# Cross-attention kernel: the value projection moved ahead of the queries, and the first queries in two alternating banks

## The reference, cut to what matters

```
q = split_heads(x @ Wq.T);  k = split_heads(ctx @ Wk.T);  v = split_heads(ctx @ Wv.T)
probs = softmax(q @ k.T / sqrt(32))
out = merge_heads(probs @ v) @ Wo.T + bo + x
```

## Time and profile before

| | |
|---|---|
| median of three executions | 444.74 us |
| profiled execution, its own time | 445.5 us |
| its span, first to last instruction | 443.7 us |
| TensorE busy | 432.1 us (97%) |
| VectorE busy | 314.3 us (71%) |
| ScalarE busy | 250.7 us (57%) |
| GpSimd busy | 228.2 us (51%) |

### The profile page before, as it was taken

How to read it: one execution, slowest core, us unless ns; L and a number is a source line. 1 busy time by engine, 2 the same in 40 slices (tenths; PEclk the granted TensorE clock), 3 DMA queues, 4 the chain that set the end, 5 groups by cost and what they waited for, 6 DMA issues and landing times.

```text
span 443.7 us, 8269 instructions
## 1 busy us (share of the span) xinstructions
PE 432.1 (97%) x2538; PEld 313.7 (71%) x2538; DVE 314.3 (71%) x509; ACT 250.7 (57%) x509; POOL 228.2 (51%) x184
## 2 busy tenths in 40 slices
PE   8989989899999999999999999999999999999996
PEld 6967665576777767776777766777777766777675
DVE  0465896877869586967869586967869586966663
ACT  1728876846565464756565464756565464755510
POOL 7403796836546373636546373636546373634440
PEclk9999989999999999999999999999999999999999
DMA  8995433535344534445344534455345443445203
GB/s 286 398 394 161 160 101 127 192 123 189 121 143 164 178 136 145 173 180 195 120 144 160 178 139 144 169 182 194 123 143 166 154 157 120 148 154 177 73 24 120
DMA packets 39615, 72.70 MB, mean 164 GB/s; under 512 B 5024, under 2 KB 6176, under 8 KB 39584
## 3 DMA queue, kind: packets, MB, share of 16 engines
q1 hardware_dynamic: 28784, 52.62, 33.2%
q10 hardware_dynamic: 10800, 19.67, 13.9%
HBM read 28.81 MB, written 10.49 MB: 89 GB/s over the span
## 4 chain that ended last, share of the span: by engine, by line
PE 91%; DVE 3%; ACT 2%; issue 1%; DMA 1%; POOL 1%; DVEq 0%; ACTq 0%; POOLq 0%
PE ps_q L676 30%; PE ps_o L676 26%; PE ps_s L722 9%; PE ps_pv L729 6%; PE ps_m L708 6%; PE ps_den L734 4%; PE ps_m L773 1%; DMA q_packed<-mxT 1%; PE ps_s L647 1%; PE ps_m L713 1%; PE ps_o L660 1%; PE ps_q L773 1%; ACT p_f L415 1%; PE ps_q L639 1%; DVE x_f L573 1%
## 5 line engine op out<-in xcount | busy, mean ns | idle before, releaser
L325 POOL TENSOR_TENSOR p_lo<-p_f,p_hi 77x512 f16<-77x512 f32 x120 | 147.7, 1236 | 169.6 <-ACT p_hi L419 169.6
L415 ACT ACTIVATE p_f<-ps_s 77x512 f32<-77x512 f32 x160 | 95.0, 593 | 47.4 <-PE ps_s L722 47.4
L419 ACT ACTIVATE p_hi<-ps_s 77x512 f16<-77x512 f32 x160 | 93.9, 587 | 1.0 <-PE ps_den L734 0.8
L534 DVE TENSOR_REDUCE mx<-ps_m 128x4 f32<-128x308 f32 x160 | 68.8, 471 | 18.0 <-PE ps_m L708 17.5
L676 PE MATMUL ps_q<-x_hi,wq_hi 128*128 128x512 f32 x200 | 79.9, 399 | 0.0
L676 PE MATMUL ps_q<-x_hi,wq_lo 128*128 128x512 f32 x200 | 78.5, 393 | 0.0
L676 PE MATMUL ps_q<-x_lo,wq_hi 128*128 128x512 f32 x200 | 78.5, 392 | 0.0
L527 DVE TENSOR_TENSOR q_lo<-ps_q,q_hi 128x512 fp32r<-128x512 f32 x40 | 27.6, 690 | 68.7 <-ACT q_hi L398 68.7
L398 ACT CAST q_hi<-ps_q 128x512 fp32r<-128x512 f32 x40 | 23.4, 585 | 91.8 <-PE ps_q L676 91.8
L676 PE MATMUL ps_o<-attn_hi,wo_hi 128*128 128x512 f32 x170 | 69.5, 409 | 0.0
L676 PE MATMUL ps_o<-attn_lo,wo_hi 128*128 128x512 f32 x170 | 66.9, 394 | 0.0
(11 more groups left out here) (105 smaller groups left out, 602.5 us busy)
## 6 DMA issues: line engine op xcount, KB each, us to landing
q_packed<-q_hi SPq DMA_DIRECT2D x80, 256.0 KB, 2.5
x_f<-in_x SPq DMA_DIRECT2D x40, 256.0 KB, 3.1
q_packed<-q_lo SPq DMA_DIRECT2D x40, 256.0 KB, 3.2
x_res<-in_x ACTq DMA_DIRECT2D x35, 256.0 KB, 2.8
out<-out_sb ACTq DMA_DIRECT2D x35, 256.0 KB, 2.6
wk_sb<-in_wk SPq DMA_DIRECT2D x8, 320.0 KB, 5.2
wv_sb<-in_wv SPq DMA_DIRECT2D x5, 512.0 KB, 10.9
wq_sb<-in_wq SPq DMA_DIRECT2D x5, 320.0 KB, 9.0
```

The costliest lines, as they stand in the source:

```text
L325: nc.gpsimd.tensor_tensor(p_lo[:, i, :], p_f[:, i, :], p_hi[:, i, :], ALU.subtract).then_inc(plo_pool, 1)
L415: nc.scalar.activation(p_f[:, i, :], ps_s[i % 2][0:L, :], ACT.Exp, scale=SCALE).then_inc(pf_done, 1)
L419: nc.scalar.activation(p_hi[:, i, :], ps_s[i % 2][0:L, :], ACT.Exp, scale=SCALE).then_inc(phi_done, 1)
L534: nc.vector.tensor_reduce(mx[:, g % RS, :, tt], ps_m[tt % 2][:, 0:HG * L].rearrange("p (h k) -> p h k", k=L), AX_X, ALU.max).then_inc(max_ ...
```

## The change

All five groups of v are projected directly behind the keys, each into a bank of its own (ps_m0, ps_m1, ps_q, ps_o, ps_pv), with their scaling, transposes and splitting interleaved; vT gets two buffers. The queries of (0, 0) come behind them. The DMA order puts two groups of Wv ahead of Wq's first group and the other three behind the first block of x. ScalarE and VectorE do the key split first at the start, then the first group of Wq. For pairs 0 to 7 the queries alternate between ps_q and ps_o. In the filling steps whose query group isn't group 0, the query chunks are spread: chunk 0 before the maxima's scores, chunk 1 behind them, chunk 2 behind the first scores, chunk 3 behind the second pair of maxima's scores, chunk 4 behind `transpose_max`. ScalarE does `q_high` ahead of the last exponentials in the filling steps. Nothing else is changed: `query_group` and the places where Wq's further groups are split remain.

```diff
@@ -75,10 +75,6 @@
...
         return isinstance(t, int) and t * G + g <= G
-
-    def value_group(t, g):
-
-        return (nth(t, g) + 1,) if isinstance(t, int) and -1 <= nth(t, g) < G - 1 else ()
...
@@ -190,7 +186,7 @@
...
             ctx_sb = sb("ctx_sb", [P, CC, BL], F32, start_up)
-            vT = sb("vT", [P, BL], F32, start_up)
+            vT = sb("vT", [P, 2, BL], F32, start_up)
         attn_hi = sb("attn_hi", [P, G, TB], F32R)
...
@@ -205,8 +201,14 @@
...
         ps_k = [ps_s[0], ps_s[1], ps_pv, ps_den, ps_o]
-        ps_v, ps_vt = ps_o[:, 0:BL], ps_o[0:L, 512 - B * P:512]
+        v_banks = [ps_m[0], ps_m[1], ps_q, ps_o, ps_pv]
+        ps_v = [v[:, 0:BL] for v in v_banks]
+        ps_vt = [v[0:L, 512 - B * P:512] for v in v_banks]
         ps_last = [ps_q, ps_m[0], ps_m[1], ps_o, ps_s[0]]
+
+        def query_bank(t, g):
+
+            return ps_o if isinstance(t, int) and t <= 1 and nth(t, g) < G + RS and nth(t, g) % 2 == 1 else ps_q
...
@@ -256,12 +258,19 @@
...
                 sp.dma_start(wk_sb[:, c, :], wk[:, c, :]).then_inc(wk_in[c], 16)
+
+            def load_wv(g):
+                sp.dma_start(wv_sb[:, g, :], wv[:, g, :]).then_inc(wv_in[g], 16)
+
+            load_wv(0)
+            load_wv(1)
             for g in range(G):
...
                     load_x(0, range(G))
+                    for v in range(2, G):
+                        load_wv(v)
                     sp.dma_start(bias[:, :], bo).then_inc(bias_in, 16)
-                sp.dma_start(wv_sb[:, g, :], wv[:, g, :]).then_inc(wv_in[g], 16)
             sp.wait_ge(const_done, 1)
...
@@ -389,13 +398,13 @@
...
                 nc.scalar.copy(v_hi[:, :, P * g:P * (g + 1)],
-                               ps_vt.rearrange("l (b c) -> l b c", b=B)).then_inc(vhi_done, 1)
+                               ps_vt[g].rearrange("l (b c) -> l b c", b=B)).then_inc(vhi_done, 1)
...
                     act.wait_ge(s_done, HG * (nth(*slot_before(t, g)) + 1))
-                nc.scalar.copy(q_hi[:, g % RS, :], ps_q[:, :]).then_inc(qhi_done, 1)
+                nc.scalar.copy(q_hi[:, g % RS, :], query_bank(t, g)[:, :]).then_inc(qhi_done, 1)
...
@@ -439,10 +448,17 @@
...
+            start_k()
             w_high(wq_in, wq_sb, wq_hi, wq_hi_done, (0,))
-            x_high(0, range(G))
-            start_k()
-            diagonal_k(0, range(HG))
+            x_high(0, range(0, 3))
+            v_high(0)
+            x_high(0, range(3, G))
+            v_high(1)
+            diagonal_k(0, range(0, 2))
+            v_high(2)
+            diagonal_k(0, range(2, HG))
+            v_high(3)
+            v_high(4)
...
@@ -458,17 +474,17 @@
...
                     exponentials(t, g, 2)
-                for v in value_group(t, g):
-                    v_high(v)
                 if exists(shift(t, g, 1)[0]):
                     copy_max(*shift(t, g, 1))
+                if filling(t, g):
+                    q_high(*shift(t, g, 2))
                 if exists(t):
...
                 attn_high(at, [c for c in (4,) if c in chunks])
-                if exists(shift(t, g, 2)[0]):
+                if exists(shift(t, g, 2)[0]) and not filling(t, g):
                     q_high(*shift(t, g, 2))
...
@@ -501,7 +517,7 @@
...
                 dve.wait_ge(vproj_done, g + 1)
-                nc.vector.tensor_reduce(v_scale[:, g:g + 1], ps_v, AX_X, ALU.max,
+                nc.vector.tensor_reduce(v_scale[:, g:g + 1], ps_v[g], AX_X, ALU.max,
                                         apply_absolute_value=True).then_inc(vscale_done, 1)
...
@@ -509,11 +525,13 @@
...
                 dve.wait_ge(vscale_done, 3 * g + 3)
-                nc.vector.tensor_scalar(vT[:, :], ps_v, v_inv[:, g:g + 1], None, ALU.mult).then_inc(vT_done, 1)
+                if g >= 2:
+                    dve.wait_ge(vtr_done, B * (g - 1))
+                nc.vector.tensor_scalar(vT[:, g % 2, :], ps_v[g], v_inv[:, g:g + 1], None, ALU.mult).then_inc(vT_done, 1)
...
                 dve.wait_ge(vhi_done, g + 1)
-                nc.vector.tensor_tensor(v_lo[:, :, P * g:P * (g + 1)], ps_vt.rearrange("l (b c) -> l b c", b=B),
+                nc.vector.tensor_tensor(v_lo[:, :, P * g:P * (g + 1)], ps_vt[g].rearrange("l (b c) -> l b c", b=B),
                                         v_hi[:, :, P * g:P * (g + 1)], ALU.subtract).then_inc(vlo_done, 1)
...
@@ -524,7 +542,7 @@
...
                 dve.wait_ge(qhi_done, nth(t, g) + 1)
-                nc.vector.tensor_tensor(q_lo[:, g % RS, :], ps_q[:, :], q_hi[:, g % RS, :].bitcast(F32),
+                nc.vector.tensor_tensor(q_lo[:, g % RS, :], query_bank(t, g)[:, :], q_hi[:, g % RS, :].bitcast(F32),
                                         ALU.subtract).then_inc(qlo_done, 1)
...
@@ -584,9 +602,20 @@
...
                                     AX_X, ALU.max).then_inc(mask_done, 1)
+            start_k()
             wq_low((0,))
-            x_low(0, DVE_CHUNKS)
-            start_k()
+            scale_v(0)
+            x_low(0, DVE_CHUNKS[:1])
+            scale_v(1)
+            v_low(0)
+            x_low(0, DVE_CHUNKS[1:])
+            scale_v(2)
+            v_low(1)
+            scale_v(3)
+            v_low(2)
+            scale_v(4)
+            v_low(3)
+            v_low(4)
             dve.wait_ge(bias_in, 16)
...
@@ -596,8 +625,6 @@
...
                     x_low(xt, DVE_CHUNKS[:1])
-                for v in value_group(t, g):
-                    scale_v(v)
                 if exists(shift(t, g, 1)[0]):
...
@@ -608,8 +635,6 @@
...
                     x_low(xt, DVE_CHUNKS[1:])
-                for v in value_group(t, g):
-                    v_low(v)
                 if exists(last_t):
...
@@ -651,13 +676,11 @@
...
-                if g == 0:
+                if g == RS:
                     pe.wait_ge(klo_done, G)
-                else:
-                    pe.wait_ge(vlo_done, g)
                 pe.wait_ge(wv_in[g], 16)
                 for c in range(CC):
-                    last = nc.tensor.matmul(ps_v, wv_sb[:, g, P * c:P * (c + 1)], ctx_sb[:, c, :],
+                    last = nc.tensor.matmul(ps_v[g], wv_sb[:, g, P * c:P * (c + 1)], ctx_sb[:, c, :],
                                             start=(c == 0), stop=(c == CC - 1))
...
@@ -665,7 +688,7 @@
...
                 for b in range(B):
-                    nc.tensor.transpose(ps_vt[:, P * b:P * (b + 1)], vT[:, L * b:L * (b + 1)],
+                    nc.tensor.transpose(ps_vt[g][:, P * b:P * (b + 1)], vT[:, g % 2, L * b:L * (b + 1)],
                                         ident[:, :]).then_inc(vtr_done, 1)
...
@@ -692,9 +715,11 @@
...
                         wait_chunk(xhi_done, xlo_dve, xlo_pool, t, c)
-                if 0 in chunks and exists(shift(t, g, -1)[0]):
+                if 0 in chunks and isinstance(t, int) and 2 <= nth(t, g) < G + RS:
+                    pe.wait_ge(qlo_done, nth(t, g) - 1)
+                elif 0 in chunks and exists(shift(t, g, -1)[0]):
                     pe.wait_ge(qlo_done, nth(t, g))
-                project(ps_q, wq_hi, wq_lo, x_hi, x_lo, g, chunks, ready, q_chunks)
+                project(query_bank(t, g), wq_hi, wq_lo, x_hi, x_lo, g, chunks, ready, q_chunks)
...
@@ -754,6 +779,8 @@
...
                     pe.wait_ge(outs_done, nth(t, k))
+                elif chunks[0] == 0:
+                    pe.wait_ge(qlo_done, G + RS)
                 project(out_bank(t, k), wo_hi, wo_lo, attn_hi, attn_lo, k, chunks, ready, o_chunks)
...
@@ -789,41 +816,51 @@
...
                 if (t, g) == (-1, G - 2):
-                    project_q(*query, range(G))
+                    project_v(0)
+                    project_v(1)
+                    for v in range(2, G):
+                        transpose_v(v - 2)
+                        project_v(v)
+                    transpose_v(3)
+                    pe.wait_ge(vlo_done, 3)
+                    project_q(*query, range(0, 2))
+                    transpose_v(4)
+                    project_q(*query, range(2, G))
                     return
...
                     pe.wait_ge(diag_done, HG)
-                    pe.wait_ge(klo_done, G)
-                for v in value_group(t, g):
-                    project_v(v)
-                if value_group(t, g):
-                    max_scores(max_t, max_g, 0, batch(max_t))
-                    max_scores(max_t, max_g, 1, batch(max_t))
+                    pe.wait_ge(vlo_done, G - 1)
+                if (t, g) == (0, 1):
+                    pe.wait_ge(vlo_done, G)
+                early = query[1] != 0
+                if early:
+                    project_q(*query, (0,))
+                max_scores(max_t, max_g, 0, batch(max_t))
+                max_scores(max_t, max_g, 1, batch(max_t))
+                if early:
+                    project_q(*query, (1,))
                 if (t, g) == (0, 0):
+                    project_q(*query, (2,))
                     pe.wait_ge(kpack_in, 16 * 3)
...
                     scores(t, g, 1, batch(t))
```

(18 more changed lines are left out.)

## The result

The changed kernel takes 473.0 us (median of four executions, 471.5 to 474.05) against 444.63 us before. The ratio is 1.0628, 95% interval 1.0587 to 1.0668. The direction and the four stops were forecast; the size was not: 462 was said, with 468 as the upper end of the range.

A forecast was written before the change was run, and what follows sets the result against it. TensorE, busy 97% of the span, was taken as the bound, so only the filling steps could change. To 444.7 us came 13 for the longer filling and 5 for the clock: 462.7, rounded down to 462; range 454 to 468.

The forecast's parts named there:

- The wait for Wq: Chunk 0 of the next query group waits for Wq's split: four stops, two of 2.3 us, two of 3.0, together 10.6.
- The transposed maxima: transpose_max waits for maxima: 1.0 us in (0, 1), (0, 2), (0, 4), (1, 0), plus 1.5 in (-1, 4) and (0, 0) together.
- The start: Five v blocks and transpositions ahead of the queries, 0.4 us for a late vT: queries of (0, 0) end at 32.5 us.
- The last stretch: Steps (0, 4) and (1, 0), from 79.0 to 99.5 us; values(0, 4) to values(1, 0) a chain of 7.5 us.
- Step (0, 3): Scores start at 72.1 us, x_low takes 1.5 us each, chunk 1 and maxima wait some 0.4; step ends at 79.0.
- The clock: In the fill, three stretches at the lower clock behind stops, 1.7 us each: +5 us, bounds 0 and +10.
- (b): Same stops in the filling steps, but the clock stays up: 454 to 458.5 us; chance 0.25.
- (c): Clock down over most of the fill, by repeated stops or bank changes: 473 us; chance 0.09.
- (d): Weights' wait in the filling steps costs nothing, up to 7.7 us go: 437 to 441 us; chance 0.04.

The follow-up runs named there:

- a1: The changed kernel with groups 1 to 4 of Wq split one step earlier, group 1 between the last groups of v: 458.25 us.
- o1: The kernel before with only the new order of the filling steps, v in its old steps and all queries in one bank: 480.08 us.
- a2: The changed kernel with 44 useless matmuls added where TensorE waits for Wq's groups 1 to 4: 467.97 us.
- a4: The changed kernel with GpSimd's three x_low of block 1 held until VectorE has done its two: 469.29 us.
- a3: The changed kernel with the old order of the filling steps, v still up front and the banks still alternating: 453.53 us.
- d1: a3 with Wq split one step earlier and GpSimd's second and third x_low of block 1 held until VectorE has done its two: 451.46 us.
- e1: The kernel before with groups 1 to 4 of v projected from only two of the eight context chunks: 445.29 us.
- c1: a1 with GpSimd's second and third x_low of block 1 held until VectorE has done its two: 452.51 us.

## Why the prediction failed, step by step

**The wait for Wq: right.** Stops of 2.29, 2.25, 3.42 and 3.43 us against 2.3, 2.3, 3.0 and 3.0, at the forecast place. a1 takes them away and 14.75 us with them; o1 shows that the order alone makes them.

**The transposed maxima: right.** 4.2 us in five waits, where 5.5 were counted.

**The start: 1.1 us too early.** The third Wv group comes late (1.06 us idle at 22.75); I had put all of 0.4 on vT and nothing on the transfer. The wait belongs partly to this one execution: in the traces of a2 and a4, whose start is the same, it is 0.42 and 0.25 us, and the queries of (0, 0) end near 32.4 us, as forecast. The last stretch was right as a sum: from the end of step (0, 3), by the timeline 92.43 us, to 112.89 are 20.5 us, as summed (79.0 to 99.5), with two errors of half a microsecond inside that cancel.

**Step (0, 3): the term for x_low was mis-sized; the step took 5.3 us more.** I took VectorE's and GpSimd's x_low at 1.5 us each side by side, as before, and "some 0.4" of waiting. VectorE's two took 7.49 us, the stop 3.57, and the clock fell behind it.

**The clock: the largest error.** The mechanism was named, three stretches at 1.7 us, +5. There were five, with 3.4 to 6.5 us of TensorE's busy time in each. By the marks of the timeline, the actual step less the forecast one: +1.4 us after the stop at 35.94, +2.4 after the one at 54.46, +2.3 after the one at 67.93, at most 1.8 of the 5.3 in (0, 3) (half of the busy time in that stretch), and about 1.6 after values(1, 0): near 9.5 where 5 were forecast. I had priced a stretch by the single one in the old trace, and that one followed an idle of 1.27 us; behind idles of 3.4 us TensorE ran 5.0 and 5.4 us at the low clock. The length of the idle doesn't set that of the stretch: behind 3.57 us it was 3.7, behind the 2.01 at 110.42 it was 6.5, and behind the 2.25 at 44.36 there was none. For the first three, the marks give 6.1 us and a2 at least 5.0, near 6.4 by its trace.

Sum of the misses on the profiled span: 28.0 measured, 18 forecast. Start 1.1, longer stops 0.8, x_low some 3.5, clock some 4.5: 9.9 together.

**The rivals.** (b), full clock, is refuted by the PEclk rows and a2. (c) gave 473 and met the time by luck: it had 15 us for the clock, where 9.5 were lost to it, and nothing beyond the 13 us of stops for x_low, the longer stops and the start. The clock was low in stretches behind stops and not over most of the fill, and no run shows a part of the bank changes in it: a1 holds the full clock over them, and o1 loses it with one bank. The section on psum-queue depth-cycling in the Trainium skill's "TensorE: Matmul & The Clock Gate" ties its swing to short idles of the engine between groups of matmuls as the banks go round; here the idles lowered the clock and the banks by themselves did not. (d) is refuted by the four waits.

**What the prediction didn't see** is that v in the steps was worth keeping. It counted v's removal as neutral. a3, d1 and e1 show that v's matmuls stood where TensorE would otherwise wait for q_high, the exponentials and the maxima. After all else is mended d1 is still about 6 us above the kernel before, of which some 4 us are left for v's move and 1.9 for the order of steps (0, 4) and (1, 0); dropping 6 us of v's matmuls gains nothing (e1). From d1 to c1, which has the new order with the same mends, the medians differ by 1.0 us and the intervals of the ratios overlap, so a price of the order by itself isn't shown.

What stays open is what brings the low clock in some executions of one and the same kernel and not in others, since one execution of each is traced. No run tells the new order of the loads or the second bank apart from the rest of these 4 us.

## What to carry to other kernels

When a piece of work is taken off the head of a step, list what ran under its cover: here the split of the next weights, the rounding of the queries and the exponentials, each of which turned into a wait. When a consumer is moved forward, its producers have to be moved with it, and the ones that stand behind other work in their own queue are found only by following that queue. Price an idle of TensorE of several microseconds at more than its length: here 11.4 us of stops brought 13.8 us of work at half rate with them, 5 to 7 us of loss. And compare the clock of a traced execution with that of the others before a stretch in it is priced into their median.

## What the runs showed of the hardware

A subtraction of two SBUF tiles on VectorE (128 x 512, float32) takes 0.69 to 0.73 us with GpSimd quiet, some 1.5 us in the kernel before beside GpSimd's equal work, and in the changed kernel 5.9 us for the first of two: it started at 80.49 and ended only behind four instructions of GpSimd that ran back to back from 80.64, each as fast as with VectorE out of the way (1.26 us for one x_low, as in a4). A p_low of GpSimd (79.51, 1.17 us) was still running when VectorE's began. a1, with the same order of starts, shows 5.92 us again. All instances of the tile in that window, with min/median/max in ns:

```profile
L325 POOL TENSOR_TENSOR x_lo<-x_f,x_hi x3: 1257/1266/1280, 80.6 to 83.1; 128x512 fp32r<-128x512 f32 x3
L540 DVE TENSOR_TENSOR x_lo<-x_f,x_hi x2: 1639/3781/5923, 80.5 to 86.3; 128x512 fp32r<-128x512 f32 x2
```

The Trainium skill ("SBUF — State Buffer", section "Who interferes with whom") says that such a VectorE instruction and a GpSimd instruction that reads SBUF contend for a shared pair of ports, held for a whole instruction, and that the loser blocks. This trace agrees, and adds that the loser can lose several times in a row. Which of the two patterns comes, 1.5 us each or one starved, was not forced by an experiment; in both kernels x_low began on both engines within 0.5 us of each other, in the changed one on VectorE first, in the one before on GpSimd.
